# Projection steps of a two-attention network issued in two halves, with one new table of slots for the finishing and the preparing work

## The chip, the cores and the metric

The program runs on one core of one Trainium2 chip. The metric is the device time of one execution in microseconds (us), as the median of several executions. The profile shown is one execution of its own, and its time is given beside the median.

## What is computed

The input is eight sequences of 512 rows and 256 columns. Each goes through four blocks, each added to its input after a layer norm: plain attention (16 heads of 16, biases), a feed-forward block made of a tree of 255 gates and 256 leaves, causal attention with rotary position codes, and the same feed-forward block again.

```python
x = x + _L0_attn_a_ref(_layernorm(x), qkv_w, qkv_b, out_w, out_b)        # softmax over all keys
x = x + _L0_ffn_ref(_layernorm(x), Wq, routers, leaf_keys, leaf_values, Wout_w, Wout_b)
x = x + _L0_attn_b_ref(_layernorm(x), Wq, Wk, Wv, Wo)                    # rotary codes, causal softmax
x = x + _L0_ffn_ref(_layernorm(x), Wq, routers, leaf_keys, leaf_values, Wout_w, Wout_b)
```

The feed-forward block computes `gate = sigmoid(x Wq' routers')`, multiplies gates or their complements along each path of the tree, and multiplies the 256 leaf probabilities by a matrix. The kernel folds its weights once at the start (`gate_w`, `leaf_w`).

## The kernel before

**Phases and slots.** One phase is one attention of one sequence, so there are 16 phases: 0, 1, 2, 4, 6, 8, 10, 12 are plain and 3, 5, 7, 9, 11, 13, 14, 15 causal (`causal(n)`). A phase has 64 slots, one for each head and block of 128 keys. Each engine runs its own copy of the same program, slot by slot, and the engines meet at semaphores. Nothing schedules at run time; the order is written out by tables.

**The core of a slot** (`core`). TensorE (PE) does the score matmul of the unit that lies `LEAD = 24` slots ahead into one of three PSUM banks (`ps_max`), for VectorE (DVE) to reduce it to a maximum (`largest`, line 785). From slot 40 on these units belong to the next phase, so the stacked operands of that phase (`q_stack`, `k_stack`) must have landed by then. PE then does this slot's matmul in the other orientation (`by_key`, `ps_key`, two banks, line 1058), whose result ScalarE (ACT) exponentiates (line 699). In every fourth slot PE multiplies four finished tiles by the values (`mixed`, line 1082). In causal phases the score matmul gets a second matmul that adds a mask to the last 128 keys (line 1026), and GpSimd (POOL) clears the upper triangle of the exponentials. Sixteen slots apart come `turn_out` (slots 8, 24, 40, 56) and `turn_max` (10, 26, 42, 58), with DVE work behind each.

**The work around it.** While phase n runs, the kernel finishes phase n-1 (`turn_attended`, `project_out`, `moments`, `spread`, `normalize`, `turn_normed`, `gates`, `leaves`, `turn_leaves`, `mix`) and prepares phase n+1 (`moments` to `turn_normed`, `heads_k`, `heads_q`, rotary `products` and `rotate` if it is causal, then the split of q and k into three bf16 parts: `high`, `rest`, `middle`, `low`). A "projection step" here is one of `project_out`, `gates`, `mix`, `values`, `heads_k`, `heads_q`: eight matmul records of PE into one bank, two of each kind in a phase but for the last phases. A step stands at one slot, and there PE, then ACT or DVE, do their share of it at the end of that slot's core. Before, the tables are `FINISH_EARLY` (causal phases whose next one is plain), `FINISH_LATE` (the others), `PREPARE_PLAIN` and `PREPARE_CAUSAL`.

**Banks.** All these steps, `turn_out` and `turn_max` write two PSUM banks (`ps_work0`, `ps_work1`), handed out in turn in program order (`work_banks`). `take` makes PE wait until the reader of the bank's last user is done.

```python
            def take(bank, event):
                if bank.name in count.last_read:
                    read, n = count.last_read[bank.name]
                    pe.wait_ge(on[read], count.of(read, count.n[read] - n))
```

**The DMA queue of SyncE (SP)** is one program too. It stacks the q and k parts into `q_stack` and `k_stack` (12 DMAs each for a causal phase, 6 for a plain one), loads `x_in` and `x_again`, stores results, and moves the residual stream: `keep()` copies `x_moved` to `x_kept` and `move()` copies `x_plain` to `x_moved`, the second after a wait for the landing of the first. Both stand at `project_out` 1 of a causal phase's finish (during plain phases 4, 6, 8, 10, 12).

## Time and profile before

| | |
|---|---|
| median of 3 runs | 1312.81 us (1310.44 to 1316.8) |
| the profiled execution, its own time | 1314.0 us |
| span of the profiled execution | 1312.3 us |
| phase 0 begins | 55.3 us after the start |
| a plain phase (10) | 81.0 us |
| a causal phase (9) | 76.6 us |
| plain phases 2 to 12, causal phases 3 to 11 | 79.9 to 81.7, 76.3 to 77.1 us |
| phases 1, 13, 14 | 80.3, 75.5, 76.4 us |
| granted TensorE clock, mean | 0.959 |

Phases are counted here from PE's first `by_key` matmul of one to that of the next. The windows below are cut at such matmuls, so that each is a whole number of slots. A window's row gives for each engine the busy time and the number of instructions that begin or run in it. The last three numbers are the granted TensorE clock (1.00 is 2.4 GHz), the busy share of the DMA engines and the GB/s that they moved. PE's busy time counts the latency of the last matmul of a run, so it comes out higher than the work.

### The profile page before, as it was taken

How to read it: one execution, taken by the hardware profiler on the slowest of the kernel's cores; microseconds unless marked ns; L12 is line 12 of the kernel's file. 1: busy time of each engine (PE TensorE's matmuls, PEld its weight loads, DVE VectorE, ACT ScalarE, POOL GpSimd, SP SyncE). 2: the span in 40 equal slices, each digit the busy share in tenths (PEclk: the TensorE clock that was granted, in tenths of full speed). 3: DMA queues.
4: the chain of work that ended last, by engine and by line, in shares of the span. 5: the costliest groups of instructions: out<-in, count | busy, mean ns of one | idle time of the engine just before them, and what ended most of it. 6: DMA issues, size and time to landing. Idle time of an engine off the chain costs nothing.

```text
span 1312.3 us, 19764 instructions
## 1 busy us (share of the span) xinstructions
PE 1186.5 (90%) x6928; PEld 597.8 (46%) x6928; DVE 913.5 (70%) x2087; ACT 718.6 (55%) x1458; POOL 337.2 (26%) x386
## 2 busy tenths in 40 slices
PE   5789999898998999999899998989899899898986
PEld 3123344354444544345453454435444354544644
DVE  3767787856776668775787657786677767776643
ACT  3166655655565554755556554565545655464551
POOL 3011113212241132502314123231223216262220
PEclk9599999999999999999999998999999998999997
DMA  7250400312004130121303122041210403011000
GB/s 207 47 129 1 97 18 21 109 49 73 25 25 121 33 97 1 57 89 33 97 2 99 47 57 73 1 129 49 61 38 13 134 17 95 5 49 50 17 17 16
DMA packets 60977, 75.37 MB, mean 57 GB/s; under 512 B 6064, under 2 KB 46672, under 8 KB 60880
## 3 DMA queue, kind: packets, MB, share of 16 engines
q1 hardware_dynamic: 58768, 73.81, 20.2%
q8 instruction: 56, 0.92, 0.3%
q0 software_dynamic: 2112, 0.30, 0.1%
q14 instruction: 41, 0.34, 0.1%
HBM read 12.45 MB, written 4.19 MB: 13 GB/s over the span
## 4 chain that ended last, share of the span: by engine, by line
PE 59%; DVE 16%; issue 6%; SPq 6%; ACT 6%; DMA 5%; POOL 2%; POOLq 0%; DVEq 0%
PE ps_work L1165 15%; PE ps_out L1082 11%; PE ps_max L1023 9%; PE ps_key L1058 8%; PE ps_work L1191 8%; DVE neg_max L785 6%; SPq L446 5%; PE ps_work L1136 4%; DMA q_stack<-q_part 3%; DVE scratch L936 2%; ACT probs L699 2%; DVE scratch L908 2%; DVE scratch L939 2%; PE ps_work L1092 1%; ACT turned_block L720 1%
## 5 line engine op out<-in xcount | busy, mean ns | idle before, releaser
L785 DVE TENSOR_REDUCE neg_max<-ps_max 128x1 bf16<-128x512 f32 (+3 forms) x1024 | 566.1, 585 | 235.4 <-PE ps_max L1026 150.1
L699 ACT ACTIVATE probs<-ps_key 128x512 f32<-128x512 f32 (+3 forms) x1024 | 504.9, 518 | 354.6 <-PE ps_key L1058 347.4
L1023 PE MATMUL ps_max<-k_stack,q_stack 96*128 96x512 bf16 (+3 forms) x1024 | 357.9, 354 | 64.0 <-DVE neg_max L785 38.6
L1058 PE MATMUL ps_key<-q_stack,k_stack 97*128 97x512 bf16 (+3 forms) x1024 | 353.7, 347 | 17.0 <-ACT probs L699 7.9
L1082 PE MATMUL ps_out<-probs,v_ones 128*32 128x512 f32 (+3 forms) x2048 | 244.1, 550 | 0.6 <-POOL probs L600 0.6
L1023 PEld LDWEIGHTS ps_max<-k_stack,q_stack 96*128 96x128 bf16 x1024 | 100.7, 98 | 301.7 <-DVE neg_max L785 176.3
L600 POOL TENSOR_SCALAR_AFFINE_SELECT probs<-probs 128x512 f32<-128x512 f32 x128 | 84.0, 656 | 302.5 <-ACT probs L699 301.9
L1058 PEld LDWEIGHTS ps_key<-q_stack,k_stack 97*128 97x128 bf16 x1024 | 101.1, 99 | 126.7 <-ACT probs L699 58.0
L586 POOL DMA_DIRECT2D q_stack<-shift_rows x64 | 34.8, 544 | 397.8 <-DVE shift_rows L795 308.8
L1026 PE MATMUL ps_max<-mask_b,ident_b 128*128 128x128 bf16 x512 | 113.7, 223 | 0.0
L1136 PE MATMUL ps_work<-ident,scratch 128*128 128x128 f32 x384 | 61.4, 291 | 24.3 <-DMA a_v_bias<-in_a_v_bias 9.4
L720 ACT ACTIVATE turned_block<-ps_work 128x512 f32<-128x512 f32 x96 | 56.7, 604 | 43.0 <-PE ps_work L1136 41.8
L622 POOL TENSOR_TENSOR rstd<-variance,minus_half 128x4 f32<-128x4 f32 (+1 forms) x34 | 33.9, 998 | 176.6 <-DVE variance L891 176.6
L1082 PEld LDWEIGHTS ps_out<-probs,v_ones 128*32 128x32 f32 x2048 | 40.9, 109 | 69.3 <-issue 63.6
L1136 PEld LDWEIGHTS ps_work<-ident,scratch 128*128 128x128 f32 x384 | 45.8, 148 | 51.3 <-DVE scratch L908 25.3
L1026 PEld LDWEIGHTS ps_max<-mask_b,ident_b 128*128 128x128 bf16 x512 | 51.0, 100 | 32.1 <-issue 9.4
L1165 PE MATMUL ps_work<-gate_w,turned_block 128*128 128x255 f32 x256 | 61.5, 390 | 4.4 <-ACT turned_block L720 4.4
L1165 PE MATMUL ps_work<-leaf_w,turned_block 128*128 128x256 f32 x256 | 59.3, 380 | 1.4 <-ACT turned_block L720 1.4
L1165 PEld LDWEIGHTS ps_work<-gate_w,turned_block 128*128 128x128 f32 x256 | 48.5, 194 | 12.0 <-ACT turned_block L720 5.9
L662 POOL TENSOR_TENSOR k_part<-scratch,k_part 128x512 bf16<-128x512 f32 x32 | 41.0, 1287 | 46.7 <-ACT k_part L757 32.9
L1165 PEld LDWEIGHTS ps_work<-leaf_w,turned_block 128*128 128x128 f32 x256 | 48.2, 190 | 9.3 <-ACT turned_block L720 1.9
L642 POOL TENSOR_TENSOR scratch<-scratch,cosine 128x512 f32<-128x512 f32 x32 | 41.4, 1295 | 31.0 <-DVE scratch L955 20.5
(86 smaller groups left out, 1287.8 us busy)
## 6 DMA issues: line engine op xcount, KB each, us to landing
k_stack<-k_part SPq DMA_DIRECT2D x48, 256.0 KB
q_stack<-q_part SPq DMA_DIRECT2D x48, 256.0 KB
k_stack<-k_part SPq DMA_DIRECT2D x96, 128.0 KB
q_stack<-q_part SPq DMA_DIRECT2D x96, 128.0 KB
x_in<-in_x SPq DMA_DIRECT2D x8, 512.0 KB, 4.7
x_again<-in_x SPq DMA_DIRECT2D x8, 512.0 KB, 4.6
x_moved<-x_plain SPq DMA_DIRECT2D x7, 512.0 KB, 3.3
out<-x_causal SPq DMA_DIRECT2D x7, 512.0 KB, 3.2
```

Of the source, the lines that this page charges most:

```text
L446: sp.dma_start(dst[rows, :, :], parts[which][part][:, c, :]).then_inc(held, DMA)
L600: pool.affine_select(out=tile, in_=tile, compare_op=ALU.is_ge, fill=0.0, base=0, pattern=[[0, GROUP], [1, P]], channel_multiplier=-1)\
L699: act.activation(probs[step % RING][:, j, q0:T], ps_key[slot % 2][:, 0:T - q0], ACT.Exp, scale=SCALE).then_inc(on["exp_done"], 1)
L720: act.activation(dst[:, :, 2 * P * i:2 * P * i + 2 * P], bank[:, :].rearrange("p (k n) -> p k n", k=KC), ACT.Copy).then_inc(on["turned"], 1)
L785: dve.tensor_reduce(out=neg_max[g % 2][:, qt, j:j + 1], in_=ps_max[score_bank(n, unit)][:, 0:keys], axis=AX_X, op=ALU.max, negate=True).th ...
L1023: last = pe.matmul(dst[:, 0:keys], q_stack[n % 2][0:SPLIT_ROWS, h, P * qt:P * qt + P], k_stack[n % 2][0:SPLIT_ROWS, h, 0:keys], start=True ...
L1026: last = pe.matmul(dst[:, keys - P:keys], ident_b[:, :], mask_b[:, :], start=False, stop=True)
L1058: pe.matmul(ps_key[slot % 2][:, 0:T - q0], k_stack[n % 2][0:STACK_ROWS, h, P * kb:P * kb + P], q_stack[n % 2][0:STACK_ROWS, h, q0:T], star ...
L1082: last = pe.matmul(ps_out[COLS * j:COLS * j + COLS, q0:T], v_flat[n % 2][:, at:at + COLS], probs[step % RING][:, j, q0:T], start=(kb == 0) ...
L1136: last = pe.transpose(by_tile(bank)[:, k, P * t:P * t + P], src[:, 2 * i + t, P * k:P * k + P], ident[:, :])
L1165: last = pe.matmul(by_tile(bank)[:, t, 0:width], turned[:, k, tile], weight[:, k, 0:width], start=(k == 0), stop=(k == KC - 1))
L1191: last = pe.matmul(bank[:, :], weight[:, k, P * i:P * i + P], turned_heads[:, k, :], start=(k == 0), stop=(k == KC - 1))
```

## The change

The two finish tables become one, `FINISH`, and the prepare tables are new. Each entry now has two kinds of slots: those at which PE does its share (a pair for a projection step, one for a transposing step, none where PE has no part) and the slot at which all other engines do theirs. A projection step's matmuls go out in two halves: for `heads` the two halves of the contraction, for the others the two tiles. The first half takes the bank, the second signals. The other engines come to the step one slot after the second half. `values` goes from slots 2 and 3 or 4 to 2 to 6. SP loads `x_in` at slot 10, a phase earlier than before, for phase n+2.

```diff
-FINISH_EARLY = (
-    (1, "bias_input", 0), (3, "bias_input", 1), (9, "turn_attended", 0), (11, "turn_attended", 1),
-FINISH_LATE = (
-    (1, "bias_input", 0), (1, "bias_input", 1), (22, "turn_attended", 0), (23, "turn_attended", 1),
+FINISH = (
+    ("project_out", 0, (21, 22), 23), ("project_out", 1, (23, 24), 25),
+    ("moments", 0, (), 24), ("moments", 1, (), 26), ("spread", 0, (), 27),
+    ("normalize", 0, (), 29), ("normalize", 1, (), 30),
+    ("turn_normed", 0, (31,), 32), ("turn_normed", 1, (32,), 33),
+    ("gates", 0, (34, 35), 36), ("gates", 1, (36, 37), 38),
+    ("leaves", 0, (), 40), ("leaves", 1, (), 42), ("leaves", 2, (), 44), ("leaves", 3, (), 46), ("leaves", 4, (), 48),
+    ("turn_leaves", 0, (50,), 51), ("turn_leaves", 1, (51,), 52),
+    ("mix", 0, (53, 54), 55), ("mix", 1, (55, 56), 57),
+    ("heads_k", 0, (9, 10), 11), ("heads_k", 1, (11, 12), 13),
+    ("heads_q", 0, (13, 14), 15), ("heads_q", 1, (15, 16), 17),
...
+def matmul_schedule(n):
+
+    due = {}
+    for slots, _, step, i, m in sorted(work_of(n), key=lambda w: w[1]):
+        for part, slot in enumerate(slots):
+            due.setdefault(slot, []).append((step, i, m, part))
     return due
...
-                uses += [(step, i, m, n) for step, i, m in schedule(n).get(slot, ()) if step in BANK_STEPS]
+                uses += [(step, i, m, n) for step, i, m, part in matmul_schedule(n).get(slot, ()) if part == 0]
...
-                    if n + 1 < PHASES and not causal(n + 1):
-                        load_x(n + 1)
+                    else:
+                        load_x(1)
+                if slot == 10 and n + 2 < PHASES and not causal(n + 2):
+                    load_x(n + 2)
...
-                    pe.wait_ge(on["turned"], count.of("turned"))
-                    take(bank, "raw_ready")
-                    for k in range(KC):
+                    if 0 in parts:
+                        pe.wait_ge(on["turned"], count.of("turned"))
+                        take(bank, "raw_ready")
+                    for k in parts:
...
+                    if 1 in parts:
+                        last.then_inc(on["heads_full"], 1)
```

On PE, slots 10 to 12 of phase 2, which is plain and prepares the causal phase 3. Before (`b_k` is the weight of `heads_k`, `neg_max` that of `turn_max`):

```order
L1136 MATMUL ps_work0<-ident,scratch 128x128 x4
L1023 MATMUL ps_max1<-k_stack0,q_stack0 128x512
L1034 MATMUL ps_work1<-ident_b,neg_max1 4x128 x4
L1058 MATMUL ps_key0<-q_stack0,k_stack0 128x512
L1023 MATMUL ps_max2<-k_stack0,q_stack0 128x512
L1058 MATMUL ps_key1<-q_stack0,k_stack0 128x512
L1191 MATMUL ps_work0<-turned_heads,b_k 128x512 x2
L1191 MATMUL ps_work1<-turned_heads,b_k 128x512 x2
L1023 MATMUL ps_max0<-k_stack0,q_stack0 128x512
```

The same place, slots 9 to 11, of the changed kernel:

```order
L1210 MATMUL ps_work1<-turned_heads,b_k 128x512
L1043 MATMUL ps_max1<-k_stack0,q_stack0 128x512
L1054 MATMUL ps_work0<-ident_b,neg_max1 4x128 x4
L1078 MATMUL ps_key0<-q_stack0,k_stack0 128x512
L1210 MATMUL ps_work1<-turned_heads,b_k 128x512
L1043 MATMUL ps_max2<-k_stack0,q_stack0 128x512
L1078 MATMUL ps_key1<-q_stack0,k_stack0 128x512
L1210 MATMUL ps_work1<-turned_heads,b_k 128x512
```

`heads_k` 0 and 1 stood one behind the other in different banks; now each is two rows apart from its second half, with a slot's core between, and both use `ps_work1`, because `turn_max` took the other bank in between. The last row is the first half of `heads_k` 1.

On DVE, slots 24 and 25 of the plain phase 4 before (L805 and L808 belong to `turn_out`, L952 and L955 are `rotate_q`):

```order
L785 TENSOR_REDUCE neg_max1<-ps_max0 128x1
L805 RECIPROCAL inverse<-ps_work0 128x16
L808 TENSOR_TENSOR attended<-ps_work0,inverse 128x4x64
L952 TENSOR_TENSOR scratch<-scratch 128x512
L955 TENSOR_TENSOR scratch<-scratch 128x512
L785 TENSOR_REDUCE neg_max1<-ps_max1 128x1
L785 TENSOR_REDUCE neg_max1<-ps_max2 128x1
```

And of the changed kernel, where L898 is `moments` and L860 the addition of `project_out`:

```order
L805 TENSOR_REDUCE neg_max1<-ps_max0 128x1
L825 RECIPROCAL inverse<-ps_work0 128x16
L828 TENSOR_TENSOR attended<-ps_work0,inverse 128x4x64
L898 BN_STATS moments<-x_causal 128x6 x2
L972 TENSOR_TENSOR scratch<-scratch 128x512
L975 TENSOR_TENSOR scratch<-scratch 128x512
L805 TENSOR_REDUCE neg_max1<-ps_max1 128x1
L860 TENSOR_TENSOR x_causal<-ps_work1,x_kept 128x512
```

`moments` and the addition of `project_out` have come to the slots where `rotate_q` stands; `moments` 1, `spread` and `normalize` follow in slots 26 to 30.

On SP, one plain phase that prepares a causal one, before:

```order
L446 DMA k_stack1<-k_part2 8x16x512 x2
L446 DMA q_stack1<-q_part0 8x16x512 x6
L446 DMA q_stack1<-q_part1 8x16x512 x4
L446 DMA q_stack1<-q_part2 8x16x512 x2
L509 DMA x_kept<-x_moved 128x1024
L499 DMA x_moved<-x_plain 128x1024
L426 DMA x_again<-in_x 128x4x256
```

The same of the changed kernel:

```order
L466 DMA k_stack1<-k_part2 8x16x512 x2
L529 DMA x_kept<-x_moved 128x1024
L519 DMA x_moved<-x_plain 128x1024
L466 DMA q_stack1<-q_part0 8x16x512 x6
L466 DMA q_stack1<-q_part1 8x16x512 x4
L466 DMA q_stack1<-q_part2 8x16x512 x2
L444 DMA x_again<-in_x 128x4x256
```

`keep()` and `move()` have passed ahead of the twelve DMAs that fill `q_stack`.

## Rows read from the trace of the kernel before

**Rows 1.** The page's head: span, and PE's busy time.

```profile
span 1312.3 us, 19764 instructions
PE 1186.5 (90%) x6928; PEld 597.8 (46%) x6928; DVE 913.5 (70%) x2087; ACT 718.6 (55%) x1458; POOL 337.2 (26%) x386
```

**Rows 2.** The page's chain that ended last, by engine.

```profile
PE 59%; DVE 16%; issue 6%; SPq 6%; ACT 6%; DMA 5%; POOL 2%; POOLq 0%; DVEq 0%
```

**Rows 3.** Windows of whole phases: 0, 2 and 15.

```profile
55.30:121.10 65.80, 61.13 (x292) 18.96 (x293) 48.26 (x90) 44.29 (x81) 9.96 (x11) 0.95 0.28 65
...
201.40:283.10 81.70, 77.13 (x426) 36.49 (x426) 59.65 (x134) 48.70 (x91) 21.24 (x19) 0.98 0.18 53
...
1221.20:1279.00 57.80, 52.70 (x394) 30.26 (x394) 31.76 (x86) 33.08 (x79) 12.91 (x20) 1.00 0.06 19
```

**Rows 4.** Windows of phase 10: slots 0-11, 12-23, 24-31, 32-39, 40-63.

```profile
831.10:848.20 17.10, 16.55 (x89) 8.67 (x89) 13.48 (x32) 8.80 (x16) 3.11 (x4) 1.00 0.01 2
848.20:862.50 14.30, 13.90 (x70) 5.36 (x68) 11.17 (x17) 10.98 (x21) 11.06 (x9) 1.00 0.18 56
862.50:871.90 9.40, 8.47 (x47) 3.14 (x44) 8.91 (x15) 6.85 (x14) 4.27 (x4) 1.00 0.42 128
871.90:882.70 10.80, 8.52 (x45) 4.09 (x46) 8.38 (x21) 5.25 (x10) 1.04 (x1) 0.95 0.56 158
882.70:912.10 29.40, 28.77 (x182) 15.41 (x180) 17.84 (x51) 16.55 (x31) 2.38 (x3) 0.96 0.12 37
```

**Rows 5.** Windows of phase 9: slots 0-11, 12-23, 24-31, 32-47, 48-63.

```profile
754.50:769.70 15.20, 14.31 (x101) 8.67 (x101) 10.21 (x29) 8.83 (x19) 3.83 (x5) 1.00 0.25 70
769.70:788.20 18.50, 17.66 (x100) 9.58 (x97) 10.02 (x26) 10.97 (x24) 3.68 (x6) 1.00 0.18 46
788.20:801.70 13.50, 11.09 (x70) 6.80 (x68) 8.59 (x17) 5.61 (x15) 6.08 (x8) 0.87 0.61 154
801.70:817.10 15.40, 13.10 (x90) 5.61 (x89) 12.14 (x34) 8.20 (x20) 3.10 (x5) 0.89 0.07 17
817.10:831.10 14.00, 13.85 (x89) 6.82 (x87) 12.03 (x22) 7.32 (x18) 3.06 (x5) 1.00 0.01 1
```

**Rows 6.** The timeline of phase 10, all engines, from 873.4 us.

```profile
874.08 1.89 PE L1165 MATMUL ps_work<-b_o,turned_block 128*128 128x256 f32 x8
...
876.03 0.38 PE L1058 MATMUL ps_key<-q_stack,k_stack 97*128 97x512 bf16 x1
...
876.44 0.60 ACT L699 ACTIVATE probs<-ps_key 128x512 f32<-128x512 f32 x1 [1.52 <-PE ps_key L1058]
```

**Rows 7.** Groups by line over the run.

```profile
L952 DVE TENSOR_TENSOR scratch<-scratch 128x512 f32<-128x512 f32 x16 | 19.3, 1209 | 1.0 <-POOL scratch L642 1.0
...
L908 DVE TENSOR_SCALAR scratch<-x_plain,spread,rstd 128x256 f32<-128x256 f32 x36 | 21.9, 653 | 0.8 <-POOL rstd L622 0.8
...
L908 DVE TENSOR_SCALAR scratch<-x_causal,spread,rstd 128x256 f32<-128x256 f32 x32 | 12.1, 434 | 1.0 <-POOL rstd L622 1.0
...
L887 DVE BATCH_NORM_AGGREGATE spread<-moments 128x2 f32<-128x6 f32 x128 | 12.1, 156 | 0.4
...
L878 DVE BATCH_NORM_STATS2 moments<-x_causal 128x6 f32<-128x256 f32 x32 | 11.9, 414 | 0.0
...
L737 ACT ACTIVATE scratch<-ps_work,a_k_bias 128x512 f32<-128x512 f32 x16 | 11.0, 687 | 37.2 <-PE ps_work L1191 37.2
```

**Rows 8.** The timeline of PE at the end of slot 39 of phase 10.

```profile
881.70 0.29 PE L1023 MATMUL ps_max<-k_stack,q_stack 96*128 96x128 bf16 x1 [2.24 <-DMA q_stack<-q_part]
```

**Rows 9.** SP's queue in phase 10: issue start, issuing time.

```profile
867.49 7.88 SPq L446 DMA_DIRECT2D q_stack<-q_part  x12
876.83 0.52 SPq L509 DMA_DIRECT2D x_kept<-x_moved  x1
882.99 0.51 SPq L499 DMA_DIRECT2D x_moved<-x_plain  x1
```

**Rows 10.** The timeline of PE in phase 0, slot 32.

```profile
92.84 0.39 PE L1058 MATMUL ps_key<-q_stack,k_stack 97*128 97x512 bf16 x1 [2.97 <-DMA q_stack<-shift_rows]
```

128 lines of the change are left out of this document (70 added, 58 removed).

## Prediction

> **What bounds the kernel now.** I read the page's head first: PE is busy for 1186.5 of 1312.3 us, no other engine for over 70% [rows 1]. The chain of waits names PE for 59% and DVE for 16%, with ACT, DMA and SP's queue at 5 to 6% each [rows 2]. So PE sets the pace on the whole, and others only in places. The windows show where. In the plain phase 10, slots 12-23 take 14.3 us with PE busy for 13.9, while slots 24-31 take 9.4 with DVE busy for 8.9, and slots 32-39 take 10.8 with PE busy for only 8.5, 2.24 of the rest being one wait for `q_stack` to land [rows 4, 8]. In the causal phase 9, slots 12-23 are PE's (17.7 of 18.5) and slots 24-47 nobody's: 28.9 us with PE busy for 24.2, at a clock of 0.87 and 0.89 [rows 5]. A clock of 0.87 over 13.5 us is 3.5 us at the lower of the two levels (1.2 GHz), for which PE's matmuls cost double; both falls follow slots in which PE mostly waited. That is what a better spreading could win. What it can lose is the same: PE stands still where DVE or a bank's reader is late.
>
> **The unit prices.** The eight records of a projection step start at 874.08, and the next two matmuls of PE, a score and a `by_key`, have the second at 876.03 [rows 6]; the first of them takes 0.22 of that, so a step costs PE 1.73 us and a half 0.87. The number of steps in a phase stays as it was; only their places change. I go through a phase by stretches: take the stretch's time before, add 1.73 us for each step that comes in and take it off for each that goes (a turning step about 0.5), but only where PE is the one that fills the stretch, and add new waits.
>
> **New wait 1, the bank of `heads_k` 1.** Its first half stands at slot 11 and uses the bank of `heads_k` 0, which ACT reads in the same slot, behind that slot's exponential. PE's `by_key` of the slot starts, the exponential starts 0.41 us later and runs 0.60 [rows 6], of which about 0.5 pass before ACT's next operation starts; the copy of `heads_k` takes 0.69 [rows 7]. PE is ready 0.22 after its own matmul's start, so it waits 0.41 + 0.5 + 0.69 - 0.22 = 1.4 us. Matmuls, scores included, queue behind it, and slots 4-15 are PE's, so nothing hides it. It is paid in all 15 phases that prepare another: 20 us. Lower bound 0 (if PE is late there anyway), upper 1.6. Shorter waits of the same kind, 0.3 to 0.8 us, stand at `turn_out` 8 and `turn_max` 58, whose banks were read a slot before; I put them into the stretches.
>
> **New wait 2, DVE in slots 24-31.** In phases that prepare a causal one DVE already fills this stretch: 8.9 of 9.4 us. Two `moments` steps (four at 0.37, 1.5), `spread` (four at 0.1 and two short ones, 0.6) and four row tiles of `normalize` (1.5) come in [rows 7], while the addition of `project_out` 0 goes and that of 1 comes. That makes 12.5 us. Then POOL: one fp32 operation of DVE on SBUF is sometimes held up; `rotate` means 1.21 us where its fellow takes 0.7, `normalize` of `x_plain` means 0.65 against 0.43 of `x_causal` [rows 7]. `normalize` at 29 and 30 now meets POOL's `low_q` at 28 and 29; I add 1.2, less 0.8 for what DVE may still owe when PE leaves the stretch (three score banks): 12.9 us, against PE's own work of some 7.6. Bounds: 11.0 and 15.
> The Trainium skill, "SBUF — State Buffer", section "SBUF: two separate sides", says that DVE and POOL share one port pair as an exclusive lock, held for a whole instruction. [...]
>
> **SP's queue.** In five phases (4, 6, 8, 10, 12) `keep` and `move` now stand ahead of the q DMAs. Before, they came after them, and PE still waited 2.24 us: the last q DMA was issued at 867.49 + 7.88 = 875.4 and PE got it at 881.7, 6.3 later; from `keep`'s issue to `move`'s it took 6.2 us [rows 8, 9]. Now, from the start of slot 24: DVE has done the addition of slot 25 after 5.2 us (two reductions, `turn_out`'s share, `moments`, both `rotate`, the addition), then 6.2, 0.5, 7.9 and 4.5 to 6.3 give 24.3 to 26.1 us. PE reaches the same need after 12.9 + 9.7 = 22.6. The wait is 1.7 to 3.5 us; I take 2.3, as before. In phases 2 and 14, where no copy stands ahead, it goes, with the slow clock behind it.
>
> **The plain phase, sum (phase 10, [rows 4]).**
> Slots 0-11: 17.1. Half a step leaves (-0.9), the bank wait and a short one come (+1.4, +0.3), a gap of some 0.6 goes (PE idle for 0.55 [rows 4]): 17.3.
> Slots 12-23: 14.3. Two steps come in (+3.5), of which 1.1 fill time in which DVE and POOL (11.2 and 11.1 busy) set the pace: 16.7.
> Slots 24-31: 9.4 to 12.9.
> Slots 32-39: 10.8. One step more, a turning step more (+2.2), DVE's `moments` gone (-1.0): 12.0, the wait for `q_stack` in it.
> Slots 40-63: 29.4. Two steps leave (-3.5) and two turning steps (-1.0), the short bank waits come (+0.5): 25.4.
> Together 84.3 against 81.0: +3.3, five times: +16.5 us.
>
> **The causal phase that prepares a plain one (9, [rows 5]).**
> 0-11: 15.2. One and a half step more (+2.6), two turning steps less (-1.0), the bank waits (+1.7), 1.5 of it in time in which PE waited or only finished late (0.9 idle): 17.0.
> 12-23: 18.5. Two steps less (-3.5), `turn_attended` in (+1.0), 0.9 of idle time filled: 15.1.
> 24-31: 13.5. One and a half step less (-2.6), a turning step less, and the slow clock's share (1.7) mostly gone: 9.2, DVE (7.7 of work) close behind.
> 32-47: 15.4. Two steps come in (+3.5) and fill most of PE's waiting (2.3 idle, 1.7 of slow clock) in 32-39; four of five `leaves` now lie in 40-47, where DVE sets the pace: I take +2.1, between 0 and +3.5: 17.5.
> 48-63: 14.0 to 15.5, for two turning steps and short waits.
> Together 74.3 against 76.6: -2.3, five times: -11.5 us.
>
> **The rest.** Phase 2 (81.7 us, [rows 3]): 84.3 less the q wait and its clock, 80.7: -1. Phase 1: 0. Phases 13 and 14 have both the DVE pile and the relief elsewhere: -1 together. Phase 15 (57.8, [rows 3]) has no `heads` and no pile. PE is busy for 52.7 of it, and the 5.1 of waits lie where its steps stand close and DVE's in heaps between them; I take most as gone: -4. Phase 0 (65.8, [rows 3]): PE waits 2.97 us at slot 32 for a shift row that lay behind `q_stack` DMAs [rows 10]; q is ready eleven slots earlier now, so that and the slow clock after it (1.7) go, and the bank wait comes: -3.3. Start and end are untouched. `x_in` loads a phase earlier, off every path.
> Sum: +16.5 - 11.5 - 1 - 1 - 4 - 3.3 = -4.3 us. The profiled execution's own time is 1314.0 us, 1.7 above its span and 1.2 above the median of the runs shown; against the median I get 1308.5, said as 1308.
>
> **Rivals.**
> A, the forecast: gains and new waits nearly cancel: 1308, own range 1297 to 1320. Chance 0.42.
> B, halves run better than by my sum. The bank wait costs nothing, because PE is behind ACT, or DVE, fed every slot, loses less than its windows say: 20 us of waits go, and 1 us in each of eight piles: 1280. For it: ACT and DVE wait for PE's lumps in every stretch with two steps in a row. Against: before, where one step stood in four slots, stretches ran at the sum of PE's work already. Chance 0.28.
> C, the slower side: `q_stack` is late. If `keep` takes longer, or the addition of slot 25 comes later by 3 us because the DVE pile delays it, PE waits 6 to 7 us in place of 2.3 at slot 40 and the clock is low for longer. 5 us in five phases: 1332. It decides from a wait of about 4 us on. For it: the queue order; against: the pile delays PE as well, so both move together. Chance 0.18.
> D, the port as an exclusive lock. POOL is busy for 4.3 us in slots 24-31 [rows 4]; if all of it adds to DVE's 12.5 in place of my 0.4, the pile costs 3.4 us more in each of eight phases (2, 4, 6, 8, 10, 12, 13, 14): 1334. The means of [rows 7] say that most operations are not held up. Chance 0.12.
>
> **How the numbers follow.** Half a per cent (6.6 us) is about what a measurement of this kernel can tell from no change. Faster by more (under 1306.2): B and 0.15 of A's 0.42, 0.43. Within: 0.22 of A. Slower: C, D and 0.05 of A, 0.35. The range takes in B's, C's and D's times, 1279 to 1336; outside are the better tail of B and C with D together, under 0.2.
>
> **What would show it.** In the profile after: PE idle 1.4 us ahead of the second `heads_k`'s first half in 15 phases, released by ACT's copy (wait 1). In plain phases, DVE busy without a break from slot 24 to 31, these eight slots at 12 to 14 us, PE released by `neg_max`. A wait of PE for `q_stack` at slot 40 of phases 4 to 12 and none in 2 and 14. No wait for the shift row in phase 0. Causal phases 3 to 11 at 74 us, plain ones at 84. Wrong it is if plain phases come out under 81 (B), or if the wait for `q_stack` is over 4 us (C).

## The result: 1392 us, 5.9% slower, and the profile after

The changed kernel takes 1392.26 us in the median of 4 runs (1387.22 to 1395.92), the kernel before, beside it, 1314.8. The ratio is 1.0586, with an interval of 1.0534 to 1.0638. The profiled execution has a span of 1385.5 us against 1312.3 [rows 1]. I had said 1308, and 1336 at most.

The head of the page after, and its chain that ended last by engine:

```profile
span 1385.5 us, 19764 instructions
...
PE 1195.4 (86%) x6928; PEld 591.1 (43%) x6928; DVE 934.2 (67%) x2087; ACT 725.0 (52%) x1458; POOL 337.5 (24%) x386
...
PE 59%; DVE 21%; ACT 10%; issue 6%; DMA 2%; POOL 1%; SPq 0%; POOLq 0%; DVEq 0%
```

PE does no more work than before (1195.4 for 1186.5 us), but span less busy time is 190.1 us where it was 125.8: of 73 us, 64 are PE standing still. In the chain ACT has gone from 6 to 10% and DVE from 16 to 21%, the DMAs and SP's queue from 11 to 2% [rows 2]. So PE waits for readers on other engines, not for transfers. The clock is no part of it: its mean went up, from 0.959 to 0.970.

By phases, of the 73 us 30 are lost in the five plain phases 4 to 12, 19 in the five causal phases 3 to 11, 16 in the last three, and 12 in phases 0 to 2; the start and the end gain 4.

The windows of phase 10 after, cut at the same slots as [rows 4]:

```profile
875.40:893.70 18.30, 16.01 (x87) 8.04 (x86) 13.66 (x32) 9.01 (x16) 3.28 (x4) 1.00 0.10 31
893.70:912.20 18.50, 17.55 (x83) 7.91 (x82) 12.18 (x18) 11.61 (x22) 11.32 (x10) 1.00 0.15 46
912.20:924.60 12.40, 8.64 (x46) 3.14 (x44) 12.16 (x28) 6.62 (x12) 4.90 (x5) 0.97 0.54 176
924.60:936.90 12.30, 11.56 (x58) 5.75 (x57) 5.73 (x10) 6.22 (x12) 0.00 (x0) 0.89 0.52 139
936.90:962.20 25.30, 23.66 (x159) 11.28 (x156) 17.77 (x51) 15.71 (x29) 2.37 (x3) 1.00 0.07 23
```

And of phase 9, as [rows 5]:

```profile
793.90:811.60 17.70, 16.14 (x99) 8.77 (x99) 11.17 (x29) 9.77 (x20) 4.75 (x6) 1.00 0.01 2
811.60:831.00 19.40, 17.15 (x98) 9.62 (x95) 10.55 (x18) 11.69 (x25) 6.83 (x7) 0.91 0.74 162
831.00:840.30 9.30, 6.68 (x55) 3.51 (x52) 7.28 (x22) 2.63 (x8) 2.85 (x4) 1.00 0.01 3
840.30:857.60 17.30, 14.74 (x103) 7.70 (x100) 12.04 (x35) 9.16 (x21) 3.10 (x5) 1.00 0.00 0
857.60:875.40 17.80, 15.25 (x97) 7.57 (x96) 13.66 (x24) 8.19 (x19) 2.42 (x4) 1.00 0.00 1
```

Phase 10 has 86.8 us (before 81.0) and phase 9 has 81.5 (before 76.6); the other plain phases from 4 on have 86.2 to 86.9, the causal ones up to 11 have 79.9 to 81.5. In phase 9 PE has 1.6 to 2.6 us without work in each of the five windows. Before, it had as much only in slots 24 to 47. Both kinds lose, where I had one losing 3.3 and the other gaining 2.3.

The groups of PE's projection and turning matmuls after, by line. The last part is idle time just before them and what ended it:

```profile
L1185 PE MATMUL ps_work<-gate_w,turned_block 128*128 128x255 f32 x256 | 68.5, 391 | 12.4 <-ACT turned_block L740 12.4
L1156 PE MATMUL ps_work<-ident,scratch 128*128 128x128 f32 x384 | 65.9, 298 | 49.4 <-DVE scratch L928 27.9 <-DMA a_v_bias<-in_a_v_bias 9.4 <-DVE v_ones L1005 5.5
...
L1185 PE MATMUL ps_work<-a_o,turned_block 128*128 128x256 f32 x128 | 38.4, 427 | 8.5 <-ACT turned_block L740 8.5
L1185 PE MATMUL ps_work<-b_o,turned_block 128*128 128x256 f32 x128 | 37.0, 419 | 6.1 <-ACT turned_block L740 6.1
L1210 PE MATMUL ps_work<-turned_heads,a_k 128*128 128x512 f32 x64 | 35.1, 640 | 9.1 <-ACT scratch L757 8.4 <-ACT turned_heads L740 0.7
L1210 PE MATMUL ps_work<-turned_heads,b_k 128*128 128x512 f32 x64 | 34.4, 619 | 9.8 <-ACT scratch L755 9.7
...
L1054 PE MATMUL ps_work<-ident_b,neg_max 128*4 128x128 bf16 x256 | 24.8, 219 | 28.1 <-DVE x_plain L860 16.0 <-DVE x_causal L860 12.1
```

Three kinds of wait are new or much longer. `heads_k` waits 18.1 us for the reader of its bank (8.4 and 9.7), the one that I had priced. `turn_max` waits 28.1 us for DVE's addition to read its bank (before, its waits were 1.6 in all); I had only part of that. And `gates` and `project_out` wait 27.0 us for ACT's copy of the turned rows, `turned_block` (12.4, 8.5, 6.1; before 5.1 in all), which I had at nothing. `turn_normed` waits 27.9 us for `normalize`, where it was 8.9. Two waits shrank: PE's for score maxima from 38.6 to 17.3 us, and for `q_stack` from 25.0 to 9.3.

One wait of each of the three kinds in phase 10, from PE's timeline after:

```profile
892.58 1.10 PE L1210 MATMUL ps_work<-turned_heads,b_k 128*128 128x512 f32 x2 [1.27 <-ACT scratch L755]
...
907.62 1.13 PE L1185 MATMUL ps_work<-b_o,turned_block 128*128 128x256 f32 x4 [0.78 <-ACT turned_block L740]
...
916.39 0.38 PE L1054 MATMUL ps_work<-ident_b,neg_max 128*4 128x128 bf16 x4 [1.09 <-DVE x_causal L860]
```

ACT around the second of them:

```profile
904.46 1.16 ACT L770 ACTIVATE k_part<-scratch 128x512 bf16<-128x512 f32 x2
905.50 0.61 ACT L719 ACTIVATE probs<-ps_key 128x512 f32<-128x512 f32 x1
905.98 0.62 ACT L740 ACTIVATE turned_block<-ps_work 128x512 f32<-128x512 f32 x1
906.46 0.63 ACT L719 ACTIVATE probs<-ps_key 128x512 f32<-128x512 f32 x1
906.93 0.64 ACT L740 ACTIVATE turned_block<-ps_work 128x512 f32<-128x512 f32 x1
907.41 0.68 ACT L777 ACTIVATE k_part<-scratch 128x512 bf16<-128x512 f32 x1
```

PE's `by_key` of slot 21 stood at 906.46, and from about 906.8 the first half of `project_out` 0, which stands at that slot, was all that PE had to do. It needs the copy of `turn_attended` 1. PE had turned those rows in slot 19, but the copy is the work of slot 20 on ACT, behind that slot's exponential (906.46), and ACT was late itself, since the two operations of `high_k` (904.46) stood before the exponential and the copy of slot 19. So the rows came at 907.6.

### The profile page after: what moved, and what is told of

Read it like the earlier page. It is cut to its first block, busy times and chain, and to the rows that moved or that the text cites. A ratio compares the mean times of both kernels' runs of the same rounds, so it can differ in the third digit from the quotient of the medians.

```text
span 1385.5 us, 19764 instructions
## 1 busy us (share of the span) xinstructions
PE 1195.4 (86%) x6928; PEld 591.1 (43%) x6928; DVE 934.2 (67%) x2087; ACT 725.0 (52%) x1458; POOL 337.5 (24%) x386
## 4 chain that ended last, share of the span: by engine, by line
PE 59%; DVE 21%; ACT 10%; issue 6%; DMA 2%; POOL 1%; SPq 0%; POOLq 0%; DVEq 0%
PE ps_work L1185 14%; PE ps_out L1102 11%; PE ps_work L1210 9%; PE ps_key L1078 9%; DVE neg_max L805 8%; PE ps_max L1043 8%; ACT probs L719 5%; PE ps_work L1156 3%; DVE scratch L928 2%; PE ps_work L1112 2%; ACT turned_block L740 2%; DMA q_stack<-shift_rows 2%; DVE moments L898 2%; DVE x_plain L860 2%; PE ps_max L1046 1%
## 5 line engine op out<-in xcount | busy, mean ns | idle before, releaser
L719 ACT ACTIVATE probs<-ps_key 128x512 f32<-128x512 f32 (+3 forms) x1024 | 519.0, 518 | 609.1 <-PE ps_key L1078 605.3
L805 DVE TENSOR_REDUCE neg_max<-ps_max 128x1 bf16<-128x512 f32 (+3 forms) x1024 | 578.0, 587 | 359.9 <-PE ps_max L1046 192.5
L1043 PE MATMUL ps_max<-k_stack,q_stack 96*128 96x512 bf16 (+3 forms) x1024 | 358.4, 353 | 30.2 <-DVE neg_max L805 17.3
L1102 PE MATMUL ps_out<-probs,v_ones 128*32 128x512 f32 (+3 forms) x2048 | 238.2, 538 | 0.6 <-POOL probs L620 0.6
L1078 PEld LDWEIGHTS ps_key<-q_stack,k_stack 97*128 97x128 bf16 x1024 | 101.0, 99 | 124.5 <-ACT probs L719 49.9
L1156 PE MATMUL ps_work<-ident,scratch 128*128 128x128 f32 x384 | 65.9, 298 | 49.4 <-DVE scratch L928 27.9
L1185 PE MATMUL ps_work<-gate_w,turned_block 128*128 128x255 f32 x256 | 68.5, 391 | 12.4 <-ACT turned_block L740 12.4
L1185 PE MATMUL ps_work<-leaf_w,turned_block 128*128 128x256 f32 x256 | 68.6, 391 | 5.1 <-ACT turned_block L740 5.1
L1185 PEld LDWEIGHTS ps_work<-gate_w,turned_block 128*128 128x128 f32 x256 | 45.7, 189 | 32.3 <-ACT turned_block L740 19.1
L662 POOL TENSOR_TENSOR scratch<-scratch,cosine 128x512 f32<-128x512 f32 x32 | 43.2, 1350 | 59.8 <-DVE scratch L975 33.4
L682 POOL TENSOR_TENSOR k_part<-scratch,k_part 128x512 bf16<-128x512 f32 x32 | 37.0, 1168 | 55.4 <-ACT k_part L777 42.8
```

The costliest lines, as they stand in the source:

```text
L662: pool.tensor_tensor(dst[:, c, :], raw[which][:, c, :], factor[:, :], ALU.mult)\
L719: act.activation(probs[step % RING][:, j, q0:T], ps_key[slot % 2][:, 0:T - q0], ACT.Exp, scale=SCALE).then_inc(on["exp_done"], 1)
L805: dve.tensor_reduce(out=neg_max[g % 2][:, qt, j:j + 1], in_=ps_max[score_bank(n, unit)][:, 0:keys], axis=AX_X, op=ALU.max, negate=True).th ...
L1043: last = pe.matmul(dst[:, 0:keys], q_stack[n % 2][0:SPLIT_ROWS, h, P * qt:P * qt + P], k_stack[n % 2][0:SPLIT_ROWS, h, 0:keys], start=True ...
L1078: pe.matmul(ps_key[slot % 2][:, 0:T - q0], k_stack[n % 2][0:STACK_ROWS, h, P * kb:P * kb + P], q_stack[n % 2][0:STACK_ROWS, h, q0:T], star ...
L1102: last = pe.matmul(ps_out[COLS * j:COLS * j + COLS, q0:T], v_flat[n % 2][:, at:at + COLS], probs[step % RING][:, j, q0:T], start=(kb == 0) ...
```

## The experiments

All kernels are built from the changed kernel's code; only tables of slots differ (and which phases use them: "old finish" means the two tables of before), but in e16 and e17 also the order of SP's queue. A row reads (step, number, PE's slots for the two halves, the others' slot). "Prompt" means that the others come in the slot of the second half, or of the turning. Equal slots for both halves are a whole step. The column "not busy" is span less PE's busy time by the page's head; before it is 125.8 us, after 190.1. The clock is the mean granted one, before 0.959. The ratio is to the kernel before, measured beside each run; its median there was between 1312 and 1319 us, so medians of runs far apart in the list compare less well than ratios.

| run | tables | median, us | ratio (interval) | not busy | clock |
|---|---|---|---|---|---|
| e1 | old | 1310.54 | 0.9965 (0.9935 to 0.9994) | 124.6 | 0.961 |
| e2 | new, whole, prompt | 1333.13 | 1.0147 (1.0101 to 1.0193) | 128.6 | 0.944 |
| e3 | new, halves, prompt | 1329.06 | 1.0118 (1.0069 to 1.0168) | 127.9 | 0.949 |
| e4 | new, whole, readers late | 1335.97 | 1.0160 (1.0117 to 1.0204) | 131.8 | 0.955 |
| e5 | the change, `heads_k` 1 later | 1375.37 | 1.0480 (1.0463 to 1.0498) | 169.8 | 0.956 |
| e6 | the change, turning prompt | 1358.98 | 1.0363 (1.0326 to 1.0401) | 161.8 | 0.961 |
| e7 | the change, projection prompt | 1376.6 | 1.0487 (1.0452 to 1.0522) | 159.8 | 0.950 |
| e8 | old finish whole, new prepare in halves, prompt | 1304.11 | 0.9937 (0.9922 to 0.9951) | 125.6 | 0.978 |
| e9 | new finish in halves, old prepare whole, prompt | 1352.22 | 1.0308 (1.0258 to 1.0358) | 148.4 | 0.945 |
| e10 | old, halves, prompt | 1325.68 | 1.0105 (1.0063 to 1.0147) | 133.0 | 0.957 |
| e11 | e3, finishing 2 slots later from 31 | 1340.76 | 1.0222 (1.0173 to 1.0272) | 130.9 | 0.950 |
| e12 | e8, two waits mended | 1309.66 | 0.9966 (0.9938 to 0.9994) | 123.2 | 0.971 |
| e13 | e3, finishing off slots 24-31 | 1375.11 | 1.0461 (1.0429 to 1.0494) | 160.9 | 0.954 |
| e14 | old finish, new prepare, whole | 1288.22 | 0.9783 (0.9760 to 0.9805) | 107.9 | 0.972 |
| e15 | as e8 | 1312.38 | 0.9967 (0.9939 to 0.9994) | 126.8 | 0.976 |
| e16 | e13, SP's copies behind q | 1350.27 | 1.0211 (1.0161 to 1.0261) | 131.7 | 0.946 |
| e17 | e16, whole | 1325.54 | 1.0045 (1.0020 to 1.0070) | 124.5 | 0.953 |
| e18 | as e14 | 1285.8 | 0.9756 (0.9720 to 0.9793) | 109.4 | 0.974 |

**Halves, late readers, tables (e1 to e4).**

```diff
 # e2: whole, prompt        e3: halves, prompt         e4: whole, readers late
-    ("heads_k", 1, (11, 12), 13), ("turn_normed", 0, (31,), 32),
+    ("heads_k", 1, (12, 12), 12), ("turn_normed", 0, (31,), 31),   # e2
+    ("heads_k", 1, (11, 12), 12), ("turn_normed", 0, (31,), 31),   # e3
+    ("heads_k", 1, (12, 12), 13), ("turn_normed", 0, (31,), 32),   # e4
```

> Code of the changed kernel with the old tables written in its form: both halves of a step at its old slot, readers at the same slot, x_in loaded at slot 10 a phase earlier. Nothing of the work around the core stands elsewhere than before. If the loss sits in the tables and in the halves alone, it runs as the kernel before: 1313 us, within 5. If the earlier load of x_in or the new loop costs something, it is 1325 or more.

> The new tables, but each projection step whole at the slot of its second half, and every reader (ACT or DVE) at that same slot, as before the change, also behind the turning steps. Theory 1 (readers that stand a slot late make PE wait at the next user of the bank or of the data, 0.7 to 1.3 us at slots 7, 11, 21, 25, 34, 57): most of that goes, 1315 to 1330. Theory 2 (the halves themselves cost, by breaking runs of matmuls): the same gain, so this run alone does not tell 1 from 2. Theory 3 (the places of the new tables: DVE's pile in slots 24 to 31 and the wait for normalize at 31): it stays at 1360 or more.

> The new tables with the halves, but readers at the slot of the second half (of the turning steps: at their slot) instead of one later. Theory 1 (late readers): about as fast as the whole steps with readers at the same slot, 1315 to 1335, and PE's waits at 11, 25 and 57 mostly gone. Theory 2 (halves cost): stays near 1380. Theory 3 (places): 1360 or more, with the wait at 31 still in it.

> The new tables, each projection step whole at the slot of its second half, readers a slot later as in the changed kernel. The bank is taken a slot later, so the wait at slot 11 should go and those at 25 and 57 stay. Theory 1: 1370 to 1380, since only the wait at 11 (1.2 us in 15 phases, 18 us) goes. Theory 2: 1320 to 1335. Theory 3: 1365 or more.

The new code with the old tables is as fast as before (e1), so the cost is in the tables. Against e2, halves alone give -0.3 points of the ratio and late readers alone +0.1, neither apart from zero by the intervals. Both together are the change, at +4.4 points. The loss is an interaction: the first half starts a slot earlier, the reader comes a slot later, and each pair loses two slots of distance where one would still have been free. In e3 the waits of the three kinds shrink, as PE's groups by line show:

```profile
L1247 PE MATMUL ps_work<-gate_w,turned_block 128*128 128x255 f32 x256 | 68.2, 390 | 1.4 <-ACT turned_block L802 1.4
...
L1247 PE MATMUL ps_work<-b_o,turned_block 128*128 128x256 f32 x128 | 35.3, 404 | 0.8 <-ACT turned_block L802 0.7
...
L1116 PE MATMUL ps_work<-ident_b,neg_max 128*4 128x128 bf16 x256 | 24.8, 219 | 9.2 <-DVE x_plain L922 5.7 <-DVE x_causal L922 3.5
```

From 12.4 to 1.4, from 6.1 to 0.8 and from 28.1 to 9.2 us.

That halves alone cost nothing here is a sum of two things. From e2 to e3 PE's waits for banks grow by 15.3 us (`turn_max` from 0 to 9.2, `heads_k` from 0 to 6.1), while those for score maxima fall from 40.6 to 31.4 and those for exponentials from 14.6 to 9.2.

**Which pair (e5 to e7).** e5 moves `heads_k` 1 and all of the preparing behind it a slot on. e6 makes only the turning steps' readers prompt, e7 only the projection steps'.

```diff
-    ("heads_k", 1, (11, 12), 13), ("heads_q", 0, (13, 14), 15),
+    ("heads_k", 1, (12, 13), 14), ("heads_q", 0, (14, 15), 16),    # e5
-    ("turn_attended", 1, (19,), 20), ("project_out", 0, (21, 22), 23),
+    ("turn_attended", 1, (19,), 19), ("project_out", 0, (21, 22), 23),    # e6
+    ("turn_attended", 1, (19,), 20), ("project_out", 0, (21, 22), 22),    # e7
```

> The changed kernel with heads_k 1, both heads_q and all that follows them one slot later, so that the first half of heads_k 1 stands at slot 12, behind a bank whose reader stands at 11. It removes the one wait that the prediction priced (1.4 us, 1.1 to 1.35 measured at slot 11 in 15 phases, 18 us). If the waits add up and only go away where they are mended: 1392 less 18 and the slow clock untouched, 1370 to 1380. If the stall is only passed on to the next bank or the next copy: 1385 to 1392.

> The changed kernel, but ACT's copies behind the four kinds of turning step (turn_attended, turn_normed, turn_leaves) stand at the turning step's own slot instead of one later; projection steps keep halves and late readers. It shortens the data path turning step to copy to first half (PE's waits at 19, 21, 34, 53) and not the banks of the projection steps (11, 25, 57). If the data path made the extra over the forecast: 1392 less 3 us in 15 phases and some slow clock, 1335 to 1350. If the banks did: 1380 to 1390.

> The complement: the changed kernel with the readers of the projection steps at the slot of their second half, the copies of the turning steps still a slot late. It mends the banks (PE's waits at 7, 11, 25, 57, some 3.5 to 4 us a phase) and not the data path. If banks are most of it: 1392 less 55 and more, 1330 to 1340. If the data path: 1370 to 1380. If both share it as the waits of the profile after say (bank 55, data 35): 1340 and 1360 for the two runs.

e5 gives back 17 us of medians (14 by the ratios), near the measured 18.1 of its wait. e6 gives back 33 (29 by the ratios), more than the 27 of the waits for `turned_block`; e7 gives back 16 (13) and leaves those waits. 33 and 16 are 49 of the 63 between the change and e3. In time that PE stands still the two do add up: 28.3 us less in e6 and 30.3 in e7, of 62.2 in e3. What is missing in the medians is e7's clock, which falls from 0.970 to 0.950, so that PE is busy for 1209.0 us in place of 1195.4.

**Which table (e8, e9).** Prompt readers in both. e8 has the old finish tables, whole, and the new prepare tables in halves; e9 has the new finish table in halves and the old prepare tables, whole.

```diff
-    ("normalize", 0, (), 29), ("normalize", 1, (), 30),            # FINISH
+    ("normalize", 0, (), 44), ("normalize", 1, (), 44),            # e8, FINISH_LATE of before
-    ("heads_k", 0, (9, 10), 11), ("heads_k", 1, (11, 12), 13),     # PREPARE_CAUSAL
+    ("heads_k", 0, (11, 11), 11), ("heads_k", 1, (11, 11), 11),    # e9, as before
```

> The old finish tables (FINISH_EARLY and FINISH_LATE, whole steps) with the new prepare tables in halves, readers at the slot of the second half. The split kernel with prompt readers and both new tables has 1329. If the 18 us that it lies above the kernel before come from the single finish table (DVE's pile in slots 24 to 31 and the wait for normalize at 31, 28 us of PE idle in it): 1305 to 1315. If they come from the prepare tables: 1325 or more.

> The changed kernel with the single FINISH table (halves at its slots, every reader at the second half's or the turning step's own slot) and the prepare tables of before, whole. Together with the run that had only the new prepare tables (1304, 0.994 of before) it splits the 1.2% that the new tables cost with prompt readers (1329). Theory 1, the finish table carries it: normalize in slots 29 and 30 stands behind the rotary products on DVE, PE waits for it at slot 31 (28 to 29 us in all); then this kernel takes 1325 to 1340 and shows that wait in nearly every phase. Rival, it takes both tables (the pile is made by the new prepare table meeting the new finish table): 1305 to 1315.

The finish table carries the loss that e3 keeps, the prepare tables none of it. e9 came out worse than both theories had it: the new finish table costs 3.1% with the old prepare tables and, by e3 over e8, 1.8% with the new ones. Both figures have halves in the new finish table against whole steps in the old ones. e2 and e14 below compare whole steps with whole steps, with prompt readers and the new prepare tables in both, and there the single finish table costs 3.7% (1.0147 against 0.9783): of the 44.3 us between their spans, 20.7 are PE standing still and 23.6 longer PE work at a lower clock (0.944 against 0.972).

**Halves in the old tables (e10).**

```diff
-    ("gates", 0, (49, 49), 49), ("gates", 1, (49, 49), 49),
+    ("gates", 0, (48, 49), 49), ("gates", 1, (48, 49), 49),
```

> The tables of before, every projection step in two halves, the first one slot earlier than the step stood, the second and the reader at its old slot. Is halving worth anything by itself, without a reader a slot late? Theory 1: the bank is taken a slot earlier, which costs nothing as long as two steps in the same bank are two slots apart; gates 0 and 1 at one slot, mix 0 and 1 at one slot and heads 0 and 1 at one slot now need a second bank in the slot before: 1308 to 1318. Rival, halves fill PE's idle time beside DVE: under 1300. Rival, each half pays again for a bank wait: over 1325.

Here halves alone cost 1.4% (1.0105 to 0.9965). The time, 1325.68, is that of the rival in which halves pay again for their banks, but the trace doesn't show that mechanism: PE's waits for banks are those of e1 (`turn_max` 1.6 us in both, `heads_k` none). Of the 16.2 us between the spans 8.4 are PE standing still, in small parts at several places, and 7.8 longer PE work. What costs it stays open. Halves alone also cost 1.9% in e15 against e14 and 1.7% in e16 against e17, so "halves are free" holds only for e3 against e2.

**The pile in slots 24 to 31 (e11, e13, e16, e17).** e11 moves the readers of `normalize` and all the finishing behind them two slots on. e13 moves `moments`, `spread` and `normalize` out of the stretch and what follows them to slots 39 to 58, in all phases but the causal ones that prepare a plain one, and phase 15.

```diff
-    ("turn_normed", 0, (31,), 31), ("gates", 0, (34, 35), 35), ("mix", 1, (55, 56), 56),
+    ("turn_normed", 0, (33,), 33), ("gates", 0, (36, 37), 37), ("mix", 1, (57, 58), 58),   # e11
-    ("moments", 0, (), 24), ("moments", 1, (), 26), ("spread", 0, (), 27), ("normalize", 0, (), 29),
+    ("moments", 0, (), 32), ("moments", 1, (), 33), ("spread", 0, (), 34), ("normalize", 0, (), 36),   # e13
```

> As the kernel with the new tables, halves and prompt readers (1329), but the turning of the normalized rows and all of the finishing behind it (gates, leaves, turning, mix) two slots later; normalize stays at 29 and 30. Theory 1, the 29 us of waits for normalize at slot 31 are only a matter of the distance to their reader: they fall to under 10 and the time to 1305 to 1315. Rival, DVE is what bounds slots 24 to 31 in any case (the pile of 12.4 us), and the wait only shows at another place, as a wait for the maximum of a score tile or at slot 33: 1322 to 1330.

> As the kernel with the new tables, halves and prompt readers (1329), but in the phases that prepare a causal one or have a causal one behind them, moments, spread and normalize of the finishing stand at slots 32 to 37 (before in 24 to 30), and gates, leaves and mix behind them at 41 to 58; the causal phases that prepare a plain one keep the finish table. So DVE has only the rotary products in slots 24 to 31 of plain phases. Theory 1, the 18 us that the new tables cost with prompt readers are the pile on DVE in these slots, through PE's waits and the low clock behind them: plain phases 4 to 12 fall from 83.5 to 80.5 us, and the time to 1305 to 1315. Rival, it is something else of the single finish table (the close steps of 35 to 58): plain phases stay at 83 or over, 1325 to 1335.

e11 bears out its rival in what it says, and overshoots its 1330 by 11: the wait for `normalize` went (29.2 us in e3, 3.9 here) and came back as waits for score maxima (from 31.4 to 51.0) and ahead of `mix` (from 1.5 to 13.3). e13 missed by 60 us. The pile did get shorter, but what lay under it came out. The windows of its phase 10, slots 24-31 and 32-39:

```profile
892.10:903.20 11.10, 8.19 (x43) 2.52 (x41) 9.67 (x19) 6.71 (x12) 5.10 (x5) 1.00 0.47 135
903.20:918.00 14.80, 7.71 (x41) 2.83 (x42) 7.32 (x20) 5.38 (x10) 1.03 (x1) 0.79 0.61 177
```

PE at the end of slot 39, and SP's queue before it:

```profile
916.99 0.29 PE L1132 MATMUL ps_max<-k_stack,q_stack 96*128 96x128 bf16 x1 [6.99 <-DMA q_stack<-q_part]
```

```profile
895.89 0.52 SPq L618 DMA_DIRECT2D x_kept<-x_moved  x1
902.99 0.51 SPq L608 DMA_DIRECT2D x_moved<-x_plain  x1
903.65 8.23 SPq L555 DMA_DIRECT2D q_stack<-q_part  x12
```

`keep` and `move` held the queue from 895.9 to 903.5, the twelve q DMAs were issued by 911.9, and PE got the last at 917.0. It had been ready 7 us earlier. e16 puts the two copies behind the q DMAs, where they stood before the change:

```diff
             def stack_low(which):
...
                         stack(m, which, 2)
+                        if which == "q" and 3 < n < PHASES - AHEAD and not causal(n):
+                            keep()
+                            move()
             def project_out(m, i, n, bank):
                 count.add("x_ready")
-                if i == 1 and causal(m) and n < PHASES - AHEAD:
-                    keep()
-                    move()
```

> The kernel that has moments, spread and normalize of the finishing out of slots 24 to 31 (1375, with a wait of 7 us for q_stack at slot 39 of five plain phases), and the two copies of the residual stream, keep and move, taken behind the q DMAs on SP in plain phases 4 to 12, where they stood before the change. Theory 1: with the pile gone the q DMAs behind keep and move are what comes last, so the wait of 7 us and the low clock behind it go: plain phases from 90 to 92 us down to 81 to 83, and the time to 1310 to 1325. Rival, q lands late for another reason: the wait stays over 4 us and the time over 1355.

> The same, but every projection step whole at its second half's slot. With the old finish tables the whole steps were 1.8% better than the halves (1288 against 1312), with the single finish table in its own places 0.3% worse. Theory 1, halves cost where their first half meets in one slot a turning step that takes the other bank or its own (a slot earlier than the whole step): this kernel has fewer such meetings and takes 1295 to 1310. Rival, it is no matter here: within 4 us of the kernel with halves.

In e16 SP issues q from 893.2 to 901.1, `keep` comes behind, and PE waits 1.97 us in place of 6.99:

```profile
906.42 0.23 PE L1132 MATMUL ps_max<-k_stack,q_stack 96*128 96x128 bf16 x1 [1.97 <-DMA q_stack<-q_part]
```

The queue order is shown: 25 us of medians (33 by the ratios), and the waits of the five phases fall from between 4.7 and 7.2 us to between 1.7 and 2.2. But e16 has 1350, not 1310 to 1325, so taking the pile away doesn't take the cost of the single finish table away. The moved steps made slots 40 to 63 longer (31.6 us in phase 10, against 24.3 in e3), and the low clock came there too; slots 24 to 63 together take 50.5 us in e16 and 50.4 in e3. With whole steps (e17) the same places take 1325.5: 25 us less than with halves, so the rival of e17 falls, but 15 us over its theory.

**Halves or slots, and the best version (e12, e14, e15, e18).**

```diff
-    ("leaves", 2, (), 36), ("leaves", 3, (), 37), ("leaves", 4, (), 39), ("turn_attended", 0, (22, ), 22),
+    ("leaves", 2, (), 37), ("leaves", 3, (), 38), ("leaves", 4, (), 40), ("turn_attended", 0, (21, ), 21),   # e12
-    ("heads_k", 0, (9, 10), 10), ("heads_k", 1, (11, 12), 12),
+    ("heads_k", 0, (10, 10), 10), ("heads_k", 1, (12, 12), 12),     # e14
```

> The kernel with the old finish tables and the new prepare tables in halves with prompt readers (1304, 0.994), and two places mended where its trace shows PE waiting: in causal phases leaves 2, 3 and 4 stand a slot later (a wait of 1.54 us at slot 39 in five phases for a maximum that DVE reduces behind the leaves), and in the late finish table turn_attended 0 and 1 stand a slot earlier (0.73 us at slot 24 in six phases, where turn_out takes a bank that ACT reads in slot 23). If these waits are what they seem, 0.7 x 6 + 1 x 5 = 9 us go: 1295. Rival, the time is DVE's and only moves: 1302 to 1305.

> Old finish tables, new prepare tables, but every projection step whole at its second half's slot, readers at the same slot. Beside the same kernel with halves in the new prepare tables (0.994 of before) it tells whether the gain of that kernel is of the halves or of the slots. Theory 1, of the slots (heads one step in two slots, in place of two in one): 1302 to 1307, as with halves. Rival, of the halves: 1308 to 1315.

> The kernel with the old finish tables and the new prepare tables in halves with prompt readers once more, with more rounds, since its gain (0.994) is as small as half a per cent. Theory 1, the gain stands: 1300 to 1308, ratio 0.991 to 0.996, with the clock low for some 60 us in place of 106. Rival, it was the day: ratio 0.997 to 1.003.

> Old finish tables, new prepare tables, whole steps at the second half's slot, readers at the same slot, once more on another chip: the best version so far (0.978 of before). Theory: 1284 to 1292, ratio 0.975 to 0.982. Rival, part of it was the day: ratio 0.985 to 0.995.

e12 gained nothing over e8, against its theory: the mended waits moved. In phase 10 the 0.73 us at slot 23 went, one of 0.75 for a score maximum came there, and one at slot 27 grew from 0.78 to 1.54. e14 is the surprise, 2.2% faster than before and outside both of its expectations; e18, the same kernel, has 2.4%. Halves in the same tables (e15) have 0.3%, between its theory and its rival (e8 had 0.6%). So the slots gain and the halves lose most of it. Slots 8 to 19 of phase 9, in e14 and then in e15:

```profile
746.50:765.20 18.70, 18.67 (x106) 10.20 (x105) 9.46 (x19) 11.31 (x25) 5.79 (x7) 1.00 0.33 86
```

```profile
758.50:780.40 21.90, 19.51 (x107) 10.02 (x105) 9.07 (x19) 11.62 (x25) 5.82 (x7) 1.00 0.28 74
```

Whole steps keep PE busy for 18.67 of 18.7 us; with halves it waits 2.4. PE and then ACT in slot 9 of e15 show one of the four waits:

```profile
760.01 0.60 PE L1245 MATMUL ps_work<-ident,attended 128*128 128x128 f32 x4
761.30 0.70 PE L1299 MATMUL ps_work<-turned_heads,a_k 128*128 128x512 f32 x1 [0.69 <-ACT turned_block L829]
```

```profile
760.65 0.60 ACT L829 ACTIVATE turned_block<-ps_work 128x512 f32<-128x512 f32 x1
```

`heads_k` doesn't read `turned_block`. But ACT counts all its copies on one semaphore, `turned`, and PE waits for all of them so far: `pe.wait_ge(on["turned"], count.of("turned"))`. The half at slot 9 stands behind `turn_attended` of the same slot in the old finish table, and so waits for its copy. The whole step at slot 10 comes a slot after it. The same wait, 0.69 us, stands at slot 11. The other two (0.48 and 0.54, at slots 11 and 15) are for banks that ACT still reads. In all, e15 waits 6.9 us for such copies and 8.7 for banks of `heads` that e14 doesn't wait for, and PE stands still for 18.9 us more; the rest of that I didn't trace.

## Why the prediction was wrong, by its steps

**Failed: what a moved pair does to the distance between a step and the reader of its input.** I took a moved step at its own 1.73 us and waits only for banks. In the term "12-23" of the causal phase [rows 5], 15.1 came out of PE's work alone; measured 19.4, with 1.23 us at slot 21 for ACT's copy, 0.69 at slot 20 for an exponential that ACT owed, and the clock at 0.91 behind them. In "48-63" I had "short waits" in 15.5; measured 17.8, with waits of 0.59, 0.39, 0.23 and 1.14 us at 50, 53, 55 and 57. The plain phase shows the same, smaller: "12-23" came to 16.7 and measured 18.5, and a turning step waits 0.95 us at slot 7 for the bank of `values`. The copies come at ACT's slot, one after PE turned the rows, and the first halves one slot before the whole step. This chain was nowhere in my sum. e6 gives it 33 of the 77 us between the medians. The sum was -4.3 us, and the span grew by 73.2. By phases, my sum was 31 us short in the five causal phases, 13 in the five plain ones, 21 in the last three and 16 in the first three, less 4 at start and end.

**Mis-sized: "shorter waits of the same kind, 0.3 to 0.8 us, stand at `turn_out` 8 and `turn_max` 58".** `turn_max` waits 28.1 us in all. The one at slot 26 (1.09 in phase 10) was not priced, and the one at 58, which I had at 0.3 to 0.8, is 0.77 in phase 10 and 1.14 in phase 9.

**Right: wait 1.** 1.4 us in 15 phases, 20 us forecast; 18.1 measured (1.27 in phase 10), and e5 gave back 17.

**Right in size: wait 2.** 12.9 us forecast for slots 24-31 of a plain phase, 12.4 measured, with DVE busy for 12.16. It shows as a wait for `normalize` (1.80 at slot 31) beside that for `neg_max`. But e16 shows that the finish table's cost doesn't go with this pile: off the stretch, the steps cost as much elsewhere. What e3 keeps (+1.2%) goes with the finish table (e8, e9) and mostly with a lower clock (0.949) and longer PE work at it, 1198.9 for 1186.5 us. Which of its places does that stays open.

**SP's queue.** The wait of 2.3 us that I took in phases 4 to 12 didn't come. SP's queue in phase 10 after:

```profile
916.37 0.52 SPq L529 DMA_DIRECT2D x_kept<-x_moved  x1
919.36 0.51 SPq L519 DMA_DIRECT2D x_moved<-x_plain  x1
920.02 8.49 SPq L466 DMA_DIRECT2D q_stack<-q_part  x12
```

Two terms of my sum were off, both to the good. The addition of slot 25 was done 4.0 us after the start of slot 24, not 5.2, and `move` followed `keep` by 3.0 us, not 6.2 (3.0 to 4.4 in the five phases), so that q was issued after 16.3 us in place of 19.8. And PE reached slot 40 after 24.7 us in place of 22.6, for waits that I hadn't priced. What sets the time of `keep`'s copy no run shows: in e13 it was 7.1 in phase 10. There the queue was late and PE early, and the wait was 6.99, rival C's price of "6 to 7 us". So the mechanism was right, and its absence in the change partly luck.

**The rest.** Plain phase: 84.3 forecast, 86.8 measured; causal 74.3 and 81.5. Phase 0 was to gain 3.3 and lost 2.7 (68.5 for 65.8, [rows 3]): waits of 1.35 us at slot 11, 1.49 at slot 20 for an exponential and 1.87 at slot 32, and a clock of 0.90. The last is the wait for a shift row that I had as gone; it only fell from 2.97. Phases 13 to 15 were to gain 5 us, and take 16 more. Neither sign that I had named for being wrong came (plain phases under 81 us, a wait for `q_stack` over 4): I had none for waits that weren't in the sum.

**The rivals.** B fell: no phase is under its time of before. D has no sign in the size of the pile: POOL was busy for 4.9 us in slots 24-31, and the pile came out 0.5 under my sum with 1.2 us for it. (D's own sum was off as well: 4.3 in place of 0.4 is 3.9 us a phase, not 3.4.) The Trainium skill, "SBUF — State Buffer", section "SBUF: two separate sides", has the shared ports as an exclusive lock for a whole instruction, but only between a POOL operation and an operation of DVE that is in a 2-port perf mode or, where the POOL operation reads SBUF, has two SBUF inputs. By that rule not all that DVE does is held. The trace agrees for `rotate_q`, which has two SBUF inputs: it took 1.63 us beside a POOL operation and 0.67 without one. A's own range ended at 1320. Where I was surest, in halves that cost what whole steps do, I had looked only at what each piece of PE's work costs, not at who must be done before it.

## What to carry to other kernels

Where engines meet at slots written out by hand, price a move by pairs: for each step, the slots from the work that produces its input or reads its bank to the step itself, and what stands between them. In these tables starting earlier and reading later were each free while a slot of distance was left (e3, e4) and cost 0.7 to 1.3 us a meeting when the last was used. Don't take the first as a rule: in three other pairs of kernels here halves alone cost 1.4 to 1.9%. A wait on a count that several producers share is a distance to all of them. And a cost that a profile doesn't show may lie under another: when a pile is taken away, look at which DMA comes next.
